# First attention of a gated two-layer network: values and turned probabilities as rounded parts and rests, attended in three passes

## What is computed

```python
x = x + jnp.tanh(g_xattn[0]) * _L0_xattn_ref(_layernorm(x), ctx_1024, ctx_1024, L0_xattn_W, L0_xattn_b)
x = x + jnp.tanh(g_ffn[0])   * _L0_ffn_ref(_layernorm(x), L0_ffn_Wg, L0_ffn_Wu, L0_ffn_Wd)
x = x + jnp.tanh(g_xattn[1]) * _L1_xattn_ref(_layernorm(x), ctx_1024, mask, gamma, beta, Wq, Wkv, Wout)
x = x + jnp.tanh(g_ffn[1])   * _L1_ffn_ref(_layernorm(x), wg, W, b)
```

```python
q = query @ W.T + b; k = key @ W.T + b; v = value @ W.T + b     # key = value = ctx
weights = jax.nn.softmax(q @ k.T / 16, axis=-1)
return weights @ v
```

## Time and profile before

| | |
|---|---|
| three runs, us | 1239.54, 1239.39, 1238.85; median 1239.39 |
| the profiled execution, us | 1239.74, of which the profile's span is 1238.0 |
| TensorE busy | 1212.5 us, 98% of the span |
| VectorE busy | 1059.5 us, 86% |
| ScalarE busy | 729.5 us, 59% |
| GpSimd busy | 884.2 us, 71% |
| chain that ended last | TensorE 92%, VectorE 3%, ScalarE 3%, issue 1% |
| granted TensorE clock, mean | 0.998 of full speed |

### The profile page before, as it was taken

How to read it: one execution, slowest core, us unless ns; L and a number is a source line. 1 busy time by engine, 2 the same in 40 slices (tenths; PEclk the granted TensorE clock), 3 DMA queues, 4 the chain that set the end, 5 groups by cost and what they waited for, 6 DMA issues and landing times.

```text
span 1238.0 us, 18431 instructions
## 1 busy us (share of the span) xinstructions
PE 1212.5 (98%) x6152; PEld 992.5 (80%) x6152; DVE 1059.5 (86%) x1775; ACT 729.5 (59%) x1509; POOL 884.2 (71%) x833
## 2 busy tenths in 40 slices
PE   7999999999999999999999999999999999999998
PEld 5778888888888888888888888888888887787775
DVE  5897899999999999999999999999999874767546
ACT  2465566666666666666666666666666535545643
POOL 3744788888888888888788888888888626443435
PEclk9999999999999999999999999999999999999999
DMA  4020200001100000000000000011000330010131
GB/s 140 26 94 1 95 26 27 26 27 43 34 26 26 26 26 26 26 26 26 27 26 26 26 26 26 27 43 34 26 26 1 129 111 1 19 35 2 35 100 64
DMA packets 42366, 48.28 MB, mean 39 GB/s; under 512 B 4239, under 2 KB 40143, under 8 KB 42015
## 3 DMA queue, kind: packets, MB, share of 16 engines
q1 hardware_dynamic: 38720, 43.07, 10.5%
q0 software_dynamic: 1440, 3.41, 0.7%
q10 hardware_dynamic: 2111, 0.63, 0.2%
HBM read 37.36 MB, written 10.29 MB: 38 GB/s over the span
## 4 chain that ended last, share of the span: by engine, by line
PE 92%; DVE 3%; ACT 3%; issue 1%; DMA 0%; POOLq 0%; ACTq 0%; POOL 0%; DVEq 0%
PE bank L1325 25%; PE bank L1327 25%; PE bank L1326 25%; ACT PC L1068 2%; PE bank L1572 2%; PE bank L1563 2%; PE bank L1725 1%; PE bank L1742 1%; PE bank L1287 1%; PE bank L1269 1%; DVE nmC L2119 1%; PE bank L1547 1%; PE bank L1231 1%; PE bank L1675 1%; PE bank L1497 1%
## 5 line engine op out<-in xcount | busy, mean ns | idle before, releaser
L1325 PE MATMUL bank<-xop_hi,w_hi 128*128 128x512 f32 x896 | 348.9, 389 | 1.2 <-ACT half_g L966 1.2
L1327 PE MATMUL bank<-xop_hi,w_lo 128*128 128x512 f32 x896 | 348.6, 389 | 0.0
L1326 PE MATMUL bank<-xop_lo,w_hi 128*128 128x512 f32 x896 | 348.6, 389 | 0.0
L1976 DVE TENSOR_TENSOR hid_lo<-hid,hid_hi 128x512 fp32r<-128x512 f32 x228 | 234.8, 1054 | 4.2 <-ACT hid_hi L990 4.1
L1325 PEld LDWEIGHTS bank<-xop_hi,w_hi 128*128 128x128 f32 x896 | 168.2, 188 | 36.6 <-ACT half_g L966 1.5
L1327 PEld LDWEIGHTS bank<-xop_hi,w_lo 128*128 128x128 f32 x896 | 168.2, 188 | 35.1
L1326 PEld LDWEIGHTS bank<-xop_lo,w_hi 128*128 128x128 f32 x896 | 168.2, 188 | 34.8
L990 ACT CAST hid_hi<-hid 128x512 fp32r<-128x512 f32 x228 | 140.8, 622 | 63.5 <-PE bank L1327 38.2
L1325 PE MATMUL bank<-hid_hi,wd_hi 128*128 128x512 f32 x344 | 134.1, 390 | 0.6 <-DVE hid_lo L1976 0.6
L1326 PE MATMUL bank<-hid_lo,wd_hi 128*128 128x512 f32 x344 | 133.8, 389 | 0.0
L1327 PE MATMUL bank<-hid_hi,wd_lo 128*128 128x512 f32 x344 | 133.8, 389 | 0.0
(11 more groups left out here) (273 smaller groups left out, 2610.0 us busy)
## 6 DMA issues: line engine op xcount, KB each, us to landing
raw_gu<-in_L_ffn_Wg_dram SPq DMA_DIRECT2D x32, 256.0 KB, 2.7
raw_gu<-in_L_ffn_Wu_dram SPq DMA_DIRECT2D x32, 256.0 KB, 3.2
raw_d<-in_L_ffn_Wd_dram SPq DMA_DIRECT2D x32, 256.0 KB, 3.6
slots<-empty_row SPq DMA_DIRECT2D x1, 2080.0 KB, 10.6
xr<-slots SPq DMA_DIRECT2D x8, 260.0 KB, 4.2
x_res<-in_x_dram SPq DMA_DIRECT2D x4, 512.0 KB, 5.0
x_mid<-x_res SPq DMA_DIRECT2D x1, 2048.0 KB, 8.9
x_res<-x_mid SPq DMA_DIRECT2D x4, 512.0 KB, 5.4
```

Of the source, the lines that this page charges most:

```text
L1325: mm(ps, w, a, start=start, stop=False, skip_group_check=True)
L1326: mm(ps, w, a_low, start=False, stop=False, skip_group_check=True)
L1327: return mm(ps, w_low, a, start=False, stop=True, skip_group_check=True)
L1976: nc.vector.tensor_tensor(out=hid_lo[n % 2][h][:], in0=hid[h][:], in1=hid_hi[n % 2][h][:].bitcast(F32), op=ALU.subtract).then_inc(lo_ready ...
```

## The change

The values are kept as `V0_hi`, rounded by ScalarE's copy from PSUM, and `V0_lo`, which VectorE makes as the PSUM value less the rounded one, in the memory of `ctx_s`. The turned probabilities are likewise `PTA_hi` and `PTA_lo`, one buffer each in place of two. `a_attend` takes three products per half of keys, so 24 instead of 8 per chunk, and waits for `a_pT_lo` as well; TensorE waits for both low halves of the values (`prep_dve` 8) before the turns of chunk 2. VectorE's order gains the two subtractions of the values behind maxima 0, and `a_pT_low(u)` at four places. Second buffer, barriers and places are these:

```diff
-        V0 = keep.take("V0", [KH, 2 * B, D], F32)
+        V0_hi = keep.take("V0_hi", [KH, 2 * B, D], F32R)
...
+        V0_lo = Arena(nc, sa.at, end).take("V0_lo", [KH, 2 * B, D], F32R)
         ctx_s = sa.take("ctx_s", [KH, 2 * B, D], F32)
...
-        PTA = sa.take("PTA", [KH, 2, 2, CH], F32)
+        PTA_hi = sa.take("PTA_hi", [KH, 2, CH], F32R)
+        PTA_lo = sa.take("PTA_lo", [KH, 2, CH], F32R)
...
-                    nc.scalar.copy(PTA[:, u % 2, k, :], bank[PT_PS[k]][0:KH, :]).then_inc(a_pT, 1)
+                    nc.scalar.copy(PTA_hi[:, k, :], bank[PT_PS[k]][0:KH, :]).then_inc(a_pT, 1)
...
-                nc.scalar.copy(V0[:, 2 * i:2 * i + 2, :].rearrange("p k d -> p (k d)"), bank[V0_PS[i]][0:KH, :]).then_inc(prep_act, 1)
+                nc.scalar.copy(V0_hi[:, 2 * i:2 * i + 2, :].rearrange("p k d -> p (k d)"), bank[V0_PS[i]][0:KH, :]).then_inc(prep_act, 1)
...
             def a_attend(u):
                 pe.wait_ge(a_pT, 2 * u + 2)
+                pe.wait_ge(a_pT_lo, 2 * u + 2)
                 for j in range(CT):
                     if u > 0 and j % 2 == 0:
                         pe.wait_ge(a_res, 2 * u - 1 + j // 2)
+                    ps, ts = bank[AV_PS[j // 2]][:, j % 2 * D:(j % 2 + 1) * D], slice(j * P, (j + 1) * P)
                     for k in range(2):
-                        ins = mm(bank[AV_PS[j // 2]][:, j % 2 * D:(j % 2 + 1) * D], PTA[:, u % 2, k, j * P:(j + 1) * P],
-                                 V0[:, u // CB * 2 + k, :], start=k == 0, stop=k == 1)
+                        v = u // CB * 2 + k
+                        mm(ps, PTA_hi[:, k, ts], V0_hi[:, v, :], start=k == 0, stop=False)
+                        mm(ps, PTA_hi[:, k, ts], V0_lo[:, v, :], start=False, stop=False)
+                        ins = mm(ps, PTA_lo[:, k, ts], V0_hi[:, v, :], start=False, stop=k == 1)
...
             pe.wait_ge(prep_act, 5)
+            pe.wait_ge(prep_dve, 8)
...
+            def a_pT_low(u):
+                for k in range(2):
+                    dve.wait_ge(a_pT, 2 * u + k + 1)
+                    nc.vector.tensor_tensor(out=PTA_lo[:, k, :], in0=bank[PT_PS[k]][0:KH, :], in1=PTA_hi[:, k, :].bitcast(F32),
+                                            op=ALU.subtract).then_inc(a_pT_lo, 1)
...
             a_maxes(0)
+            for i in range(2):
+                dve.wait_ge(prep_act, 4 + i)
+                vs = slice(2 * i, 2 * i + 2)
+                nc.vector.tensor_tensor(out=V0_lo[:, vs, :].rearrange("p k d -> p (k d)"), in0=bank[V0_PS[i]][0:KH, :],
+                                        in1=V0_hi[:, vs, :].rearrange("p k d -> p (k d)").bitcast(F32), op=ALU.subtract).then_inc(prep_dve, 1)
             ln1_variances(3)
+            a_pT_low(0)
             ln1_normed(3)
             a_maxes(1)
             a_add(0)
+            a_pT_low(1)
             ln2_variances(0)
...
             a_add(1)
+            a_pT_low(2)
             ln2_variances(1)
...
             a_add_half(2, 0)
             x_first_sum(nc.vector, dve, 0)
+            a_pT_low(3)
             a_add_half(2, 1)
```

More of the change, by code:

```diff
@@ L144, in flamingo_kernel @@
     C_VALUES = 2 + HB // 2
-    PREP_DVE = 6
+    PREP_DVE = 8
     PREP_PE = 10
@@ L367, in flamingo_kernel @@
                              "a_out_ps", "a_res", "a_ln2", "a_x2T_ps"))
-        x_raw_ready = sem("x_raw_ready")
+        x_raw_ready, a_pT_lo = sem("x_raw_ready"), sem("a_pT_lo")
         x_sum_ready, x_hi_ready, x_lo_ready = (
```

## The result

The changed kernel takes 1249.03 us (median of 4 runs, 1248.23 to 1249.38) against 1239.47 for the kernel before (4 runs, 1238.85 to 1239.8): ratio 1.0072, interval 1.0056 to 1.0088. It is 9.6 us slower. The forecast had said slower, 1244.0 with a range up to 1247.5; the time lies outside it.

A forecast was written before the change was run, and what follows sets the result against it. TensorE bounds the main loop, TensorE and VectorE share the first attention's path. The profiled 1239.74 us plus 4.4 of shift made 1244.1, less 0.35 for the runs' median 1243.8, stated as 1244.0 us; range 1241.2 to 1247.5.

The forecast's parts named there:

- The bound: TensorE bounds the main loop; in the first attention VectorE is just in time, and a shift there is given back nowhere.
- TensorE's price: Each attend: 24 rounded 256-column instructions at 0.11 us, 2.65 us, so 1.0 us less for each of four chunks.
- Rival C: In the attends, a rounded 256-column instruction costs 0.228 us, an attend 5.5 us: +8, 1247.7 us; chance 8%.
- The walk: First attention, event by event with durations kept: the main loop starts 63.23 -> 67.35, turns inside it +4.4 us.
- the sum: VectorE's terms in the first attention: 6.3 us of work plus 4.3 of later waits, less 6.1 of present waits.
- rival B: VectorE's normalisations of chunks 3 and 0 miss GpSimd's work: only +1.6 to +2.5, 1241 to 1242 us; chance 14%.
- rival D: Gaps of 1.7 to 2.7 us between 44 and 68 lower TensorE's clock: up to 1.7 us, 1245.7; chance 20%.
- Rival A: VectorE's subtractions fit its 7 idle us in the first attention and TensorE keeps its savings: -3.3, 1236.1 us; chance 5%.
- the second cost: Low probabilities 3, ahead of the second half's addition on VectorE, wait for ScalarE's copy and run 60.8 to 62.0.
- step 5: From attend 2's start at 56.15 to the second half's addition, which moves 57.45 -> 62.0: +4.5 us.

The follow-up runs named there:

- e5: The changed kernel with 3, 2, 3, 5 and 3 unused products (results never read) at five places in TensorE's waits; 1244.68 us.
- e1: The kernel before with VectorE's ten subtractions, TensorE's two new waits and one buffer for turned probabilities, attends still in fp32; 1255.51 us.
- e4: The changed kernel with the low probabilities of chunk 3 moved behind the second half's addition of chunk 2 and its statistics; 1249.83 us.
- e3: The changed kernel with ten unused fp32 products in four of TensorE's waits in the first attention; 1246.37 us.
- e2: The changed kernel without any subtraction or the two waits for them, all three passes on rounded parts; 1241.93 us.
- e7: e2 with five unused products in TensorE's remaining waits; 1238.64 us.
- e11: e5 with low probabilities 3 behind the second half's addition of chunk 2, and one unused product instead of three ahead of the main loop; 1244.14 us.

## Why the prediction was wrong

**The bound** was read right: whatever the first attention loses is kept to the end, and VectorE was just in time.

**TensorE's price** was nearly right: 0.12 us against 0.11 taken, 2.97 us for the first attend at full clock (33.99 to 36.96) against 2.65. Rival C, with 5.5, is out.

**The walk** held step by step while the clock did. In e5, which entered the stage 0.59 us later, the normalisation of chunk 1 stands at 54.52 - 0.59 = 53.93 where the walk has 53.85; e5 is 5.3 us slower where the sum said 4.4. The 0.9 us left are mostly the first sum beside GpSimd: the walk had it start at 58.7, e5 has 59.42 - 0.59 = 58.8, but I had given it the 1.0 us up to ScalarE's rounding, and it took 2.00. In the changed kernel it held up to the first fall of the clock (statistics of chunk 3 at 25.77 + 0.56 = 26.3) and was 1.8 us short by the normalisation of chunk 1; the waits of 1.39 and 2.14 us stand where 1.7 and 2.3 were foreseen. Relief at the port (rival B) came in one place of the changed kernel, the normalisation of chunk 3 in 1.37 us in place of 2.89, and was lost again in the wait for TensorE behind it; in e5 the same normalisation took 2.48.

**The step that failed** is rival D, twice. First its place: I found gaps of 1.7 to 2.7 us by my own walk, had a row in which the clock fell behind gaps of 0.70, 0.46 and 0.62 us (by the same trace), and still put the fall beside the sum with 20% instead of into it. All four runs of the changed kernel have mean clocks of 0.989 to 0.994, against 0.998 or more in most runs of the kernel before. The walk also had TensorE's wait for the subtracted values, and did not take it for a gap: the profiled execution has 1.60 us there, and the first fall right behind it. Second its price: "3.4 us, costs up to 1.7" took the length of the one fall that the trace of before has. It was 3.4 and 17 us, 20.5 in all, and cost 4.3. The first fall set VectorE back by 55.62 - 53.93 = 1.7 us against e5 at the normalisation of chunk 1; the rest is the second fall, in which attend 2 and attend 3 took 5.3 us each, with the turns and the first products between. Which of the waits started each fall stays open: e1 and e4, with the same wait of 1.60 us, have no first fall in their profiled executions. The page that I cited beside it (the Trainium skill, TensorE: Matmul & The Clock Gate, "What's actually happening") says that an idle TensorE is throttled until it has been busy again. The first half agrees with the waits filled in e3 and e5. The second holds for the first fall of the changed kernel, which ended in unbroken work, and not for e2, where the rate stayed at half through 5.00 of 5 us busy.

**Rival A** fell on its second premise too, that TensorE keeps its savings: even with no subtraction at all the passes are worth 0.7 us (e7) and not 3.3.

**The low probabilities of chunk 3** ("the second cost" of step 5) do cost where they stand: 1.4 us by the traces of e5 and e11, of which about 0.9 is the place itself. The run times of the two do not part, and at the low clock the same kind of move (e4) gave nothing back.

## What to carry to other kernels

This stage of short matmuls that wait a little for each other had a clock to lose. Before adding waits of a microsecond or two to such a stage, put a fall of the clock into the sum and not beside it, with the TensorE work behind the wait at half rate; here falls lasted from 3 to 20 us. Idle time of an engine in a profile is no room for more work unless it lies where the work must stand in its queue: VectorE had 7 idle us and ten subtractions of 6.3 us cost 5.3. To part a slow clock from a late engine, fill the waits with products that nobody reads; what comes back was the clock, provided that TensorE still waits a little behind them.

## What was unexpected of the hardware

- The granted clock fell with TensorE busy 4.20 of 5 us and no wait over 0.80 us (e2, from 52 us on), and it did not return for 17 us, 5 of them without a break. Falls end differently: the changed kernel's first, at 26 us, lasted 3.4 us and ended in turns and scores, its second only in the main loop's first products (the spacing goes from 0.43 to 0.23 us between 73.2 and 74.6 us). In e1 the rate came back at about 66 us and fell again at about 70.
- Five unused products of about 0.55 us made a kernel 3.3 us faster (e2 to e7), and held its ten runs between 1237.89 and 1239.74.
- The spread of one program's runs goes with its mean clock: e2 1239.63 at 0.998 to 1245.32 at 0.992, and the kernel before itself 1238.47 at 1.000 to 1243.13 at 0.993 in 31 runs, though it mostly stays at 1239.3.
- One VectorE sum of two SBUF operands of 512 columns, the first sum, took 0.68, 1.11, 1.45 or 2.00 us in different kernels. GpSimd stood at a different point of its work each time; no run changes that alone.
